# A fused embed, attention and mixture-of-experts kernel: image 2 moved behind tile 1's first gate, image 3's maxima moved to block 5, image 1's reciprocal moved to VectorE

## The chip, the cores and the metric

The kernel runs on one core of a Trainium2 chip. The metric is the device time of one execution in microseconds (us). The engines are TensorE (PE; its weight loads are PEld), VectorE (DVE), ScalarE (ACT), GpSimd (POOL) and SyncE (SP), which here only issues transfers. Each engine works through its own list of instructions in order and waits on semaphores that other engines or transfers raise.

## The reference, cut to what matters

16 images, each of 36 patch tokens and 77 text tokens (113 in all), width 192.

```python
h = embed(x)                       # patches @ proj_w.T + proj_b
h = concat([h, txt], axis=1)       # 16 x 113 x 192
h = h + attn(layernorm(h))         # 12 heads of 16; the mask bars token i >= 1 from itself
h = h + ffn(layernorm(h))

def ffn(u):                        # u: 1808 tokens x 192
    pe = softmax(posembed @ pos_w + pos_b)
    y = moe_mlp(u, sg_w, su_w, sd_w)                       # shared expert, 384 hidden
    for i in range(16):
        f = u * pe[i] @ gate_w + gate_b                    # 192 values for each token
        weight, idx = top_k(f, 96)
        weight = softmax(weight)
        g = take_along_axis(u, idx) * weight               # 96 of the token's own columns
        y = y + moe_mlp(g, eg_w[i], eu_w[i], ed_w[i])
    yn = layernorm(y, eps=1e-6) * ln_g + ln_b
    return silu(yn @ m1_w + m1_b) @ m2_w + m2_b
```

The expensive part is the top 96 of 192 values in descending order, for 16 experts and 1808 tokens.

## The kernel before, in words

The 1808 tokens are one rest tile of 16 tokens (tile 0) and 14 tiles of 128 (tiles 1 to 14). A tile's 16 experts are taken four at a time; such a unit of work is a **block**. Block 0 is the rest tile (its 16 experts lie packed in two bands of 128 rows), blocks 1 to 56 are tiles 1 to 14 with g = 0 to 3.

**VectorE's share of a block** (`slot` in `block.vector`, L626 on): for each pair of experts, 12 rounds. A round finds, for two experts, the next eight largest values (L643), their indices (L647) and strikes them out (L649). A block has 2 x 12 rounds, block 0 has 12. After round 0 of the next block `close_block` (L624) writes the low digits of the indices: until then nobody may use block n's indices. Before a block's pair VectorE waits for its gate values (`keys`), and for `weights_ready`, that is, for the exponentials of the block two before it. Between rounds it also takes the maxima of the attention scores of later images (L593, three instructions per image); `max_after` says behind which round, as (block, pair, round).

**The rest of the pipeline.** The other engines work on a block in 16 steps (octets); (n, o) below is step o of block n. In each step TensorE makes a one-hot code from the index digits (L1269), looks tokens up with it (L1281), ScalarE copies both out (L834, L844), GpSimd multiplies them (L1113). Beside that fixed work a step may hold a gate (L1245: gate values of a later block, copied to `keys` by ScalarE at L793, the next step), an expert unit going up (L1330, L1335, L1338) or, four steps later, down (L1362), the closing of a tile, or one attention stage. At step 8 of block n-1 ScalarE takes block n's indices (`prepare`, L809 to L811); GpSimd squares them, SyncE sends them to DRAM and back into `rows`, and TensorE needs these rows at step 14 of block n-1.

**Attention.** The 15 stages of an image are embed, turn_x, q, k, v, s0 to s2 (scores), t0 to t2 (turned probabilities), mix, turn_o, proj, turn_h. The images 0 and 1, and image 2 up to its scores, run ahead of block 0 in the order of the list `FIRST`; `FIRST_MORE` says behind which stage ScalarE does a stage's second half (the squares of a layer norm, the exponentials of the scores). The rest of image 2 and images 3 to 15 stand in the steps of the blocks: `attention_steps` gives each stage the next step that is free by `FREE`, with a minimal distance (`GAP`, else 2). Tile 1 needs images 0 and 1 whole, so its first gate stands behind (1, "turn_h"); tile 2 needs image 2.

In TensorE's list the three early gates (0,1), (1,0), (1,1) of tile 1 stood behind (2, "s2"). ScalarE's (1, "turn_h") copied first to `hst` and then to `nt_gate`, which the gate reads. Image 1's softmax sums were inverted by GpSimd with a power (L1014).

SyncE's list matters at one place: in block 1's slot it loads expert weights, waits for the first unit to be down (`downed`), and only behind these loads issues the digits of block 2 (L490) and their return (L498).

## Time and profile before

| | us |
|---|---|
| median of 3 runs | 2607.87 |
| lowest and highest | 2597.53, 2609.46 |
| the profiled execution itself | 2605.05 |
| its span, first to last instruction | 2603.2 |
| mean granted TensorE clock | 0.907 |

How to read it: busy time is counted inside the span. A clock of 1.00 is 2.4 GHz, 0.50 is 1.2 GHz. Idle time of an engine is put down to what released it. The chain is followed back from the last instruction, at each step to what released it. So it names the work that a later end would need, while an idle stretch that is not on it may cost nothing.

### The profile page before, as it was taken

Reading aid. Unit: us, or ns where it says so; the run is one execution under the profiler, and the core shown is the slowest. Engines: PE = TensorE matmul, PEld = TensorE weight load, DVE = VectorE, ACT = ScalarE, POOL = GpSimd, SP = SyncE. Lnnn points to the kernel's source line nnn. Section 1 sums busy time; section 2 is a strip of 40 time slices with the busy share of each in tenths; the row PEclk is TensorE's granted clock in tenths of the full one; section 3 lists DMA queues with packets and bytes.
Section 4 is the critical chain, followed back from the end, with each engine's and each line's share of the span. In section 5 each row is a group of like instructions: output and inputs, shape, how many; then the busy total and the mean of one; then the engine's idle time right before and its main releaser. Section 6 shows DMA issues by size and latency. Waiting matters only on the chain.

```text
span 2603.2 us, 48218 instructions
## 1 busy us (share of the span) xinstructions
PE 2285.7 (88%) x11466; PEld 1244.9 (48%) x11466; DVE 2494.4 (96%) x13314; ACT 1701.2 (65%) x4090; POOL 1791.9 (69%) x2165
## 2 busy tenths in 40 slices
PE   6788989999988889889998889899889988887888
PEld 4555545454444454445544445445445454443445
DVE  5897999999999999999999999999999999999983
ACT  3354676776776667676667767667676666666563
POOL 1245777777786677777767777767768777676683
PEclk8688999988999799999899999998998988989798
DMA  3021222222221222221222122222221222121211
GB/s 107 18 56 27 53 52 61 46 50 55 53 62 44 47 58 46 57 56 44 53 52 61 45 53 50 57 50 56 51 53 49 46 50 61 43 57 46 50 50 26
DMA packets 124767, 133.58 MB, mean 51 GB/s; under 512 B 39923, under 2 KB 112638, under 8 KB 124486
## 3 DMA queue, kind: packets, MB, share of 16 engines
q1 hardware_dynamic: 123174, 128.02, 21.1%
q8 instruction: 95, 1.56, 0.3%
q14 instruction: 186, 1.52, 0.2%
q0 software_dynamic: 880, 1.62, 0.2%
q10 hardware_dynamic: 432, 0.86, 0.1%
HBM read 102.58 MB, written 27.87 MB: 50 GB/s over the span
## 4 chain that ended last, share of the span: by engine, by line
DVE 74%; PE 12%; DMA 4%; POOL 4%; ACT 3%; issue 3%; SPq 0%; DVEq 0%; ACTq 0%; POOLq 0%
DVE idx L647 26%; DVE keys L649 25%; DVE vals L643 22%; PE ps L1281 3%; DMA rows<-digit_d 2%; PE ps L1338 1%; PE ps L1362 1%; DMA digit_d<-dcode 1%; PE ps L1294 1%; PE ps L1245 1%; PE ps L1269 1%; POOL picked L1113 1%; ACT code L834 1%; DVE nmax L593 1%; PE ps L1335 1%
## 5 line engine op out<-in xcount | busy, mean ns | idle before, releaser
L1113 POOL TENSOR_TENSOR picked<-looked_s,code 128x384 f32<-128x384 f32 (+1 forms) x896 | 878.9, 990 | 456.6 <-ACT looked_s L844 455.2
L647 DVE FIND_INDEX8 idx<-vals,keys 128x8 uint16<-128x192 f32 x2712 | 943.2, 349 | 0.0
L844 ACT ACTIVATE looked_s<-ps 128x384 f32<-128x384 f32 (+1 forms) x896 | 440.6, 492 | 653.6 <-PE ps L1281 651.6
L649 DVE MATCH_REPLACE8 keys<-vals,keys 128x192 f32<-128x192 f32 x2486 | 843.4, 339 | 0.0
L643 DVE MAX8 vals<-keys 128x8 f32<-128x192 f32 x2712 | 822.3, 343 | 19.3 <-ACT keys L793 19.3
L1281 PE MATMUL ps<-code,table 128*128 128x384 f32 (+1 forms) x1824 | 839.0, 544 | 0.0
L834 ACT ACTIVATE code<-ps 128x768 f32<-128x768 f32 (+1 forms) x896 | 725.7, 810 | 69.1 <-PE ps L1269 60.4
L1269 PE MATMUL ps<-rows,codew 17*128 17x384 bf16 (+1 forms) x1824 | 320.1, 348 | 189.3 <-ACT code L834 115.0
L1269 PEld LDWEIGHTS ps<-rows,codew 17*128 17x128 bf16 x1824 | 86.9, 92 | 744.8 <-ACT code L834 374.7
L1281 PEld LDWEIGHTS ps<-code,table 128*128 128x128 f32 x1824 | 315.3, 205 | 190.6 <-issue 147.6
L1338 PE MATMUL ps<-xwt,wexp 96*96 96x128 f32 x1792 | 270.8, 299 | 35.9 <-ACT xwt L800 33.6
L1338 PEld LDWEIGHTS ps<-xwt,wexp 96*96 96x96 f32 x1792 | 220.3, 175 | 111.2 <-ACT xwt L800 47.4
L1043 POOL TENSOR_TENSOR prod_s<-gu_s 96x256 f32<-96x256 f32 x252 | 181.7, 721 | 95.7 <-ACT gu_s L886 94.9
L1294 PE MATMUL ps<-picked,place 128*32 128x384 f32 (+1 forms) x1824 | 220.3, 559 | 17.8 <-POOL picked L1113 17.8
L1362 PE MATMUL ps<-wdown,hid 96*128 96x192 f32 (+1 forms) x944 | 220.3, 362 | 3.2 <-POOL hid L1049 3.1
L647 DVE MATCH_VALUE_LOAD idx<-vals,keys 128x8 f32 x2712 | 199.3, 74 | 0.0
L1046 POOL TENSOR_TENSOR turned_s<-prod_s,tanh_s 96x256 f32<-96x256 f32 x252 | 181.5, 720 | 19.8
L1049 POOL TENSOR_TENSOR hid<-prod_s,turned_s 96x256 f32<-96x256 f32 x252 | 181.3, 719 | 19.8
L1245 PE MATMUL ps<-wgate,nt_gate 96*128 96x384 f32 x448 | 187.1, 543 | 4.4 <-ACT nt_gate L768 1.7
L1362 PEld LDWEIGHTS ps<-wdown,hid 96*128 96x128 f32 (+1 forms) x944 | 161.9, 200 | 41.5 <-issue 23.7
L649 DVE MATCH_VALUE_LOAD keys<-vals,keys 128x8 f32 x2486 | 170.6, 69 | 0.0
L886 ACT ACTIVATE gu_s<-ps 96x512 f32<-96x512 f32 x250 | 150.7, 603 | 0.0
(166 smaller groups left out, 2228.3 us busy)
## 6 DMA issues: line engine op xcount, KB each, us to landing
wexp<-in_w_exp SPq DMA_DIRECT2D x58, 576.0 KB, 4.3
wdown<-in_w_down SPq DMA_DIRECT2D x58, 576.0 KB, 4.5
digit_d<-dcode SPq DMA_DIRECT2D x56, 384.0 KB, 2.6
rows<-digit_d SPq DMA_DIRECT2D x224, 96.0 KB
table<-norm_d SPq DMA_DIRECT2D x448, 3.0 KB
patch<-in_patches SPq DMA_DIRECT2D x16, 108.0 KB, 4.7
norm_d<-hs SPq DMA_DIRECT2D x16, 84.8 KB
tok_d<-h SPq DMA_DIRECT2D x16, 84.8 KB
```

The source lines that it names most:

```text
L643: nc.vector.max(vals[:, par, e, at], from_keys[:, e, :]).then_inc(chain, 1)
L647: found = nc.vector.max_index(idx[:, par, e, at], vals[:, par, e, at], from_keys[:, e, :])
L649: nc.vector.match_replace(from_keys[:, e, :], vals[:, par, e, at], from_keys[:, e, :], NEG).then_inc(chain, 1)
L834: nc.scalar.activation(code[:, o % 4, :, 0:w], ps[:, CODE_B:CODE_B + 2, 0:w], ACT.Relu).then_inc(code_ready, 1)
L844: nc.scalar.activation(looked_s[:, o % 4, 0:w], ps[:, LOOK_B[o % 2], 0:w], ACT.Copy).then_inc(looked_out, 1)
L1113: nc.gpsimd.tensor_tensor(picked[:, o % PICKS, w], looked_s[:, o % 4, w], code[:, o % 4, 1, w], ALU.mult).then_inc(picked_ready, 1)
L1245: ins = nc.tensor.matmul(ps[:, bank, 0:2 * D], nt_gate[0:HALF + k, k, :], wgate[0:HALF + k, k, GRP * g + 2 * pair:GRP * g + 2 * pair + 2, ...
L1269: ins = nc.tensor.matmul(ps[:, CODE_B + a, w], codew[at, :], rows[at, octet(o), w], start=True, stop=True)
L1281: ins = nc.tensor.matmul(ps[:, LOOK_B[o % 2], w], table[:, o, :], code[:, o % 4, 0, w], start=True, stop=True)
L1294: ins = nc.tensor.matmul(ps[32 * q:32 * (q + 1), XG_B, w], place[:, r, :], picked[:, (QUADS * r + q) % PICKS, w], start=(r == 0), stop=(r ...
L1338: ins = nc.tensor.matmul(dst, wexp[:, e // GRP % 2, e % GRP, at:at + HALF], xwt[:, e % GRP, :], start=True, stop=True)
L1362: ins = nc.tensor.matmul(ps[0:REST if rest_tile else TILE, Y_B, 0:D], source[:, c, own], w, start=(u == 0 and x == 0 and c == 0), stop=(u ...
```

## The change

Five edits.

1. `FIRST`: image 1's embed moves from ahead of (0, "turn_x") to behind (0, "v"). Image 2's stages, which lay between those of image 1, all move behind (1, "turn_h"), and with it behind tile 1's first gate. The other three early gates now stand inside image 2 (behind its embed and turn_x). The rest tile's gate (`gate_rest`, `keys_out(0, 0, 0)`) moves from behind (0, "turn_h") to behind (1, "s0").
2. Image 2's exponentials move from the end of `FIRST` to steps 0 to 2 of block 0, so its t0 moves from (0, 0) to (0, 4); with it every stage of images 2 to 5 moves by 2 to 12 steps. For image 3: embed (0, 14) to (1, 7), s0 to s2 from (1, 13), (1, 15), (2, 1) to (2, 5), (2, 7), (2, 13). From image 6 on nothing moves.
3. `max_after`: image 2's maxima from (1, 0, 4) to (1, 0, 9), image 3's from (3, 1, 9) to (5, 0, 3), image 4's from (6, 1, 9) to (7, 0, 9), image 5's from (10, 0, 6) to (10, 1, 0).
4. Image 1's sums are inverted by VectorE behind round 8 of block 0 with a reciprocal, no longer by GpSimd.
5. ScalarE: a one-element copy ahead of all others, so that the table load no longer follows TensorE's first result; the exponential for `pe` moves from behind (0, "q") to behind (0, "k"); at (1, "turn_h") the copy to `nt_gate` comes first.

TensorE's list around tile 1's first gate (L1245 before, L1259 after; `v,probt` is image 1's mix, `wpatch,patch` an embed). Before:

```order
L1225 MATMUL ps<-v,probt 113x17 x12
L1198 MATMUL ps<-xt,wqk 128x113 x6
L1188 MATMUL ps<-ident,xn 96x113 x2
L1233 MATMUL ps<-wo,ot 113x192 x2
L1234 MATMUL ps<-h,ident 113x192
L1198 MATMUL ps<-xt,wqk 128x113 x6
L1206 MATMUL ps<-wv,xt 113x192 x2
L1188 MATMUL ps<-ident,hs 96x113 x2
L1245 MATMUL ps<-wgate,nt_gate 128x384 x2
```

After:

```order
L1239 MATMUL ps<-v,probt 113x17 x12
L1202 MATMUL ps<-ident,xn 96x113 x2
L1247 MATMUL ps<-wo,ot 113x192 x2
L1248 MATMUL ps<-h,ident 113x192
L1202 MATMUL ps<-ident,hs 96x113 x2
L1259 MATMUL ps<-wgate,nt_gate 128x384 x2
L1188 MATMUL ps<-text,ident 113x192
L1193 MATMUL ps<-wpatch,patch 36x192 x6
L1194 MATMUL ps<-bpatch,ones 113x192
```

Image 2's q, k and v are gone from between image 1's mix and the gate, and its embed follows the gate.

ScalarE's list at the same place (`hs,stat` is the square for image 1's second norm, `keys` the gate's result). Before:

```order
L780 ACTIVATE hs,stat<-h,stat 113x192
L735 ACTIVATE kz<-ps 32x3x113 x4
L739 ACTIVATE v<-ps 113x12x16
L764 ACTIVATE hst<-ps 96x226
L768 ACTIVATE nt_gate<-ps 96x2x31
L793 ACTIVATE keys<-ps 128x384
```

After:

```order
L791 ACTIVATE hs,stat<-h,stat 113x192
L772 ACTIVATE nt_gate<-ps 96x2x31
L778 ACTIVATE hst<-ps 96x226
L804 ACTIVATE keys<-ps 128x384
L820 ACTIVATE dcode<-digits 128x192
```

Five copies no longer stand ahead of the one to `nt_gate`.

TensorE's list at step (0, 14), where the first code of block 1 (384 wide) is made (`picked,place` is fixed work). Before:

```order
L1269 MATMUL ps<-rows,codew 128x384 x2
L1294 MATMUL ps<-picked,place 32x192 x4
L1174 MATMUL ps<-text,ident 113x192
L1179 MATMUL ps<-wpatch,patch 36x192 x6
L1180 MATMUL ps<-bpatch,ones 113x192
L1281 MATMUL ps<-code,table 128x192
```

After:

```order
L1283 MATMUL ps<-rows,codew 128x384 x2
L1308 MATMUL ps<-picked,place 32x192 x4
L1202 MATMUL ps<-ident,xn 96x113 x2
L1295 MATMUL ps<-code,table 128x192
```

Image 3's embed has left this step, and image 2's turn_o has come.

The diff, cut to what decides the order:

```diff
-FIRST = [(0, "embed"), (1, "embed"), (0, "turn_x"), (0, "q"), (0, "k"), (0, "v"), (1, "turn_x"), (0, "s0"), (0, "s1"), (0, "s2"),
...
+FIRST = [(0, "embed"), (0, "turn_x"), (0, "q"), (0, "k"), (0, "v"), (1, "embed"), (0, "s0"), (0, "s1"), (0, "s2"),
...
+REST_OF = STAGES[STAGES.index("t0"):]
@@ attention_steps
+        if i < AHEAD:
+            step = 3 - GAP[REST_OF[0]] + 1
         for stage in REST_OF if i < AHEAD else STAGES:
-            if stage not in ("embed", "t0") or stage == "t0" and i >= AHEAD:
+            if stage != "embed":
@@ ATT_MORE
+for _c in range(3):
+    ATT_MORE[AHEAD - 1, f"s{_c}"] = _c
@@ max_after
-    spots = {(0, 0, 2): 1, (1, 0, 4): 2}
+    spots = {(0, 0, 2): 1, (1, 0, 9): 2}
...
-        block, r = divmod(rounds, 2 * ROUNDS)
+        block, r = divmod(rounds + (ROUNDS if i == AHEAD else 0), 2 * ROUNDS)
@@ VectorE, slot
+                            if (n, pair, r) == (0, 0, 8):
+                                dve.wait_ge(misc_out, stage_out(1, "mix"))
+                                nc.vector.reciprocal(rinv[:], mix[:, :, DH]).then_inc(att_rinv, 1)
@@ ScalarE, attend_out, turn_h
+                        if i == 1:
+                            to_gate()
+                            act.wait_ge(packed, 2)
+                        nc.scalar.activation(hst[:], turn_view(i, stage), ACT.Copy).then_inc(misc_out, 1)
+                        if i == 0:
+                            to_gate()
@@ ScalarE, the list
+                nc.scalar.activation(nmax[0:1, 0:1], ones[0:1, 0:1], ACT.Copy)
...
-                    if (i, stage) == (0, "q"):
+                    if (i, stage) == (0, "k"):
                         act.wait_ge(pe_max, 1)
...
-                    if (i, stage) == (0, "turn_h"):
+                    if (i, stage) == (1, "s0"):
                         keys_out(0, 0, 0)
...
-                    if (i, stage) == (2, "s2"):
-                        for g, pair in ((0, 1), (1, 0), (1, 1)):
-                            keys_out(1, g, pair)
+                    if (i, stage) == (2, "embed"):
+                        keys_out(1, 0, 1)
+                        keys_out(1, 1, 0)
+                    if (i, stage) == (2, "turn_x"):
+                        keys_out(1, 1, 1)
@@ GpSimd, attend, mix
-                        if i:
+                        if i >= 2:
@@ TensorE, the list: the same three places as ScalarE's
```

## Rows read from the trace of the kernel before

**Rows 1.** The page's part 1: busy us (share of the span) and instructions.
```profile
PE 2285.7 (88%) x11466; PEld 1244.9 (48%) x11466; DVE 2494.4 (96%) x13314; ACT 1701.2 (65%) x4090; POOL 1791.9 (69%) x2165
```

**Rows 2.** VectorE's timeline: start, us, line, tiles, [idle before <- what ended it].
```profile
69.64 0.61 DVE L643 MAX8 vals<-keys 128x8 f32<-128x192 f32 x2
...
71.47 0.61 DVE L643 MAX8 vals<-keys 128x8 f32<-128x192 f32 x2
...
84.95 0.62 DVE L643 MAX8 vals<-keys 128x8 f32<-128x192 f32 x2 [8.31 <-ACT keys L793]
...
223.10 0.62 DVE L593 TENSOR_REDUCE nmax<-score 113x4 f32<-113x452 f32 x1 [10.93 <-ACT score L742]
229.87 0.62 DVE L593 TENSOR_REDUCE nmax<-score 113x4 f32<-113x452 f32 x1 [6.14 <-ACT score L742]
```

**Rows 3.** The chain that ended last, 131 to 240 us: start, us, what.
```profile
131.65 0.52 ACT whole L810
...
163.50 6.82 PE ps L1335 x64
...
180.23 5.32 PE ps L1362 x32
...
186.87 8.58 DMA digit_d<-dcode
...
197.38 5.00 DMA rows<-digit_d
...
204.36 10.35 PE ps L1335 x64
```

**Rows 4.** The same chain, 585 to 640 us.
```profile
625.35 0.39 ACT keys L793
625.76 0.61 DVE vals L643 x2
```

**Rows 5.** The same chain, 626 to 2545 us, grouped by line.
```profile
by line: DVE idx L647 34.6%; DVE keys L649 33.4%; DVE vals L643 28.4%; issue 1.0%; DVE nmax L593 0.8%; DVE digits L624 0.8%; PE ps L1281 0.3%; DVEq L625 0.1%; PE ps L1269 0.1%; PE ps L1338 0.1%; PE ps L1294 0.1%; PE ps L1362 0.1%; ACT code 
```

**Rows 6.** Timelines of ScalarE and VectorE at tile 3's first gate.
```profile
449.00 0.50 ACT L793 ACTIVATE keys<-ps 128x384 f32<-128x384 f32 x1
...
451.28 0.60 DVE L643 MAX8 vals<-keys 128x8 f32<-128x192 f32 x2
```

**Rows 7.** Timelines of GpSimd and ScalarE ahead of tile 1's first gate.
```profile
70.43 2.28 POOL L1014 TENSOR_TENSOR rinv<-mix,powers 113x12 f32<-113x12 f32 x1 [5.59 <-ACT mix L751]
...
79.12 0.50 POOL L1033 TENSOR_SCALAR hs<-h,stat 113x192 f32<-113x192 f32 x1
...
79.21 1.82 ACT L735 ACTIVATE kz<-ps 32x339 f32<-32x339 f32 x4 [1.09 <-PE ps L1198]
...
81.52 0.22 ACT L768 ACTIVATE nt_gate<-ps 96x62 f32<-96x62 f32 x1
```

**Rows 8.** TensorE's timeline: embed twice, a proj, a k, a score.
```profile
56.43 2.14 PE L1179 MATMUL ps<-wpatch,patch 128*36 128x192 f32 x12
...
136.67 1.62 PE L1233 MATMUL ps<-wo,ot 128*113 128x192 f32 x4
...
146.97 3.89 PE L1179 MATMUL ps<-wpatch,patch 128*36 128x192 f32 x12
...
185.46 1.59 PE L1198 MATMUL ps<-xt,wqk 128*128 128x113 f32 x12
...
195.01 0.92 PE L1214 MATMUL ps<-kz,qt 128*113 128x452 f32 x2
```

**Rows 9.** Stages: stretch, us, busy us of each engine, TensorE's granted clock, DMA.
```profile
99.00:131.00 32.00, 26.48 (x98) 16.49 (x98) 32.00 (x176) 10.20 (x26) 8.78 (x12) 0.50 0.02 3
...
152.00:202.00 50.00, 43.57 (x261) 25.28 (x259) 50.00 (x274) 26.30 (x67) 24.32 (x33) 0.93 0.27 66
202.00:223.00 21.00, 20.58 (x98) 13.52 (x99) 10.18 (x54) 4.86 (x9) 4.16 (x5) 0.52 0.10 24
223.00:626.00 403.00, 365.21 (x1885) 199.95 (x1884) 395.63 (x2122) 280.34 (x679) 302.90 (x366) 0.93 0.22 51
```

More of the change, by code:

```diff
@@ L69 @@
         2: [1, 5, 7, 9, 11, 13, 15], 3: [1, 5, 7, 9, 11, 13, 15]}
-FIRST = [(0, "embed"), (1, "embed"), (0, "turn_x"), (0, "q"), (0, "k"), (0, "v"), (1, "turn_x"), (0, "s0"), (0, "s1"), (0, "s2"),
[3 rows of a table removed]
-FIRST_MORE = {(0, "turn_x"): [(1, "embed")], (0, "s1"): [(0, "s0")], (0, "s2"): [(0, "s1"), (0, "s2")],
-              (1, "s1"): [(1, "s0")], (1, "s2"): [(1, "s1"), (1, "s2")], (2, "s2"): [(2, "s0"), (2, "s1"), (2, "s2")]}
-REST_OF = ["t0", "t1", "t2", "mix", "turn_o", "proj", "turn_h"]
+FIRST = [(0, "embed"), (0, "turn_x"), (0, "q"), (0, "k"), (0, "v"), (1, "embed"), (0, "s0"), (0, "s1"), (0, "s2"),
[3 rows of a table added]
+FIRST_MORE = {(0, "s0"): [(1, "embed")], (0, "s1"): [(0, "s0")], (1, "turn_x"): [(0, "s1"), (0, "s2")], (1, "s1"): [(1, "s0")],
+              (1, "s2"): [(1, "s1"), (1, "s2")]}
+REST_OF = STAGES[STAGES.index("t0"):]
 FIRST_BANKS = [2, XG_B, GU_B, CODE_B, CODE_B + 1, 1]
@@ L761, in attend_out, with to_gate @@
                             act.wait_ge(normt_out, 16 * i)
-                        if i == 1:
-                            act.wait_ge(packed, 2)
-                        nc.scalar.activation(hst[:], turn_view(i, stage), ACT.Copy).then_inc(misc_out, 1)
-                        if i < 2:
+                        def to_gate():
                             mine, at = (slice(REST, TOK), 0) if i == 0 else (slice(0, REST + TILE - TOK), TOK - REST)
@@ L1431, in _ @@
                         ins.then_inc(pe_mm, 1)
-                    if (i, stage) == (0, "turn_h"):
+                    if (i, stage) == (1, "s0"):
                         pe.wait_ge(pe_col_ready, 1)
@@ L1440, in _ @@
                         gate(1, 0, 0)
-                    if (i, stage) == (2, "s2"):
-                        for g, pair in ((0, 1), (1, 0), (1, 1)):
-                            gate(1, g, pair)
+                    if (i, stage) == (2, "embed"):
+                        gate(1, 0, 1)
+                        gate(1, 1, 0)
+                    if (i, stage) == (2, "turn_x"):
+                        gate(1, 1, 1)
                 pe.wait_ge(placed_w, 5 + PER // 2)
```

6 rows, old and new, of the table FIRST are left out of this document.

## The prediction, as it was put on record

> **What bounds the kernel now.** I read the page's busy shares first: VectorE is busy 96% of the span [rows 1], so at first sight only VectorE's idle time is to be had. Its own timeline shows where that lies [rows 2]: 8.31 us ahead of block 1, and 10.93 + 6.14 = 17.07 us in block 3, where it waits for image 3's scores. The change addresses both, and a reader who stops here forecasts 17 us and more.
>
> The chain of waits says something else. It has three parts. Up to 131 us it ends in VectorE, whose indices of block 1 ScalarE takes at 131.65. From there to 625.8 us it isn't in VectorE at all: it goes through TensorE, ScalarE, GpSimd and the transfers of the digits and rows [rows 3, 4], and leaves them only where ScalarE has copied tile 4's first gate values and VectorE starts block 13, at 625.76. From there to 2545 us it is VectorE in over 96% [rows 5]. The 17.07 us lie in the middle part, at 212 to 230, beside the chain and not on it. Two more rows show that VectorE may not use the time if it gets it. Tile 3's first gate values are copied at 449.00 to 449.50, and VectorE begins them at 451.28 [rows 6]: it could come 1.8 us earlier there and no more. At block 13 it is already too early. In the middle part TensorE is busy 365.21 of 403 us (91%) [rows 9]: this pipeline runs at its own pace, and VectorE's stall of 17 us has been absorbed by it before block 13. So the question is by how much the pipeline comes to block 13 earlier, not by how much VectorE does.
>
> **The change part by part.**
>
> Start, image 0. Image 1's embed and its copy leave the way of image 0's, and the table load goes ahead. I cost both at nothing up to image 0's scores, because ScalarE must copy the mask behind (0, "turn_x") in both kernels, and the mask's transfer doesn't move; what comes earlier waits there. Moving the `pe` exponential behind k saves less than 1 us of ScalarE, and image 1's turn_x and q, now ahead of image 0's t0, take about as much back.
>
> Tile 1's first gate. The reciprocal: GpSimd's power ends at 70.43 + 2.28 = 72.71 [rows 7]. VectorE's comes behind round 8 of block 0, which runs from 69.64 to 71.47 [rows 2] (so a round is 1.83 us), and with one short instruction ends by 71.7: 1.0 us earlier. It isn't 2.3 earlier, since the reciprocal must wait for its place between rounds. Then the norm that ended at 79.12 + 0.50 = 79.62 ends at 78.6, and TensorE's turn_h, about 0.6, at 79.3. The copy to `nt_gate` stood at 81.52, behind image 2's k (79.21 to 81.03), v and `hst` [rows 7]; now it follows at once, at 79.4. The gate and its copy follow in both, so VectorE, which began block 1 at 84.95, begins it 2.2 us earlier, at 82.8. Bounds: 0, if image 1 comes later by as much, and 8.31, the whole wait. I take 2.2 because every link but one is a row.
>
> Image 2 then stands behind the gate. TensorE reaches block 0 at about 101 instead of 99, but ScalarE waits for block 1's indices until 131.65 anyway, and those come with VectorE, 2.2 us earlier. The shift of the chain at 131 is -2.2.
>
> Block 0's end. At (0, 14) TensorE has waited for the rows of block 1, and everything behind is on the chain. Image 3's embed stood there, 3.89 us at half clock for its larger part [rows 8]; two short transposes replace it: -3.9. Image 2's mix comes from (0, 6) to (0, 10), ahead of that wait, which covers it.
>
> Block 1 up to the unit at step 9. proj comes in at (1, 1): +1.6 at half clock. The embed at (1, 7) takes the place of a q: 2.14 at full clock for 1.59 [rows 8], +0.6. The clock is a cost of its own. Before, the embed at 146.97 ran at half clock and the stretch from 152 on had 0.93 [rows 8, 9]. Without the embed the first steps of block 1 may stay at half clock. Until the gate and the proj are through that is 0 to 4 us; I take 2. Here SyncE issues block 2's digits only when the unit that ends at 185.55 is down [rows 3], so what the pipeline gains up to there is kept by the transfers (186.87 to 202.4). Shift there: -2.2 - 3.9 + 1.6 + 0.6 + 2.0 = -1.9.
>
> Blocks 1 to 10. Image 3's k, v and s0 stood ahead of the wait for block 2's rows and now stand behind it: 1.59 + about 0.8 + 0.92 = +3.3 [rows 8]. Stages of images 3 to 5 that fall into steps 9 to 13 of a block run while rows are awaited and cost nothing; block 8 gets such a pair. I count half of the 3.3: +1.7. Bounds 0 and 3.3. All other stages of images 3 to 5 are done by block 10 in both kernels, and image 6 stands where it stood.
>
> VectorE's maxima of image 3, in block 5, will find their scores ready, and ScalarE, which wants them at (3, 5), finds VectorE ahead by more than 10 us, since VectorE has 17.07 us more. Their 3 x 0.62 us of work remain. The reciprocal adds some 0.2 us of VectorE work ahead of block 13: nothing.
>
> Sum at block 13: -1.9 + 1.7 = -0.2 us. VectorE's list behind it is the same in both, so the end moves by the same. From the profiled execution, 2605.05 us (span 2603.2 and 1.85 around it), the forecast is **2605 us**. The median of the runs shown, 2607.87, is 2.8 above that execution, which lies inside their range; I don't correct for it.
>
> **The rivals.**
>
> A, faster: TensorE's clock stays up. The stretch from 202 to 223 ran at 0.52 with TensorE busy 20.58 of 21 us [rows 9], directly on the chain. If the new order keeps the clock up there, half of it goes, -10.3, and the 2.0 above aren't paid: -12.5, 2592.5 us. VectorE would allow it: its own limit is 17.07 + 2.2 lower, 2585.8. For it: TensorE now comes into block 0 straight from image 2's scores, without a wait. Against: the half clock at 202 follows on a wait for rows that doesn't go away, and TensorE was busy 26.48 of 32 us from 99 to 131 at 0.50 [rows 9], so being busy did not bring the clock back. The Trainium skill, "TensorE: Matmul & The Clock Gate", section on the HAM clock gate, says that the default is the throttled state and that activity releases the throttle. By that rule block 0 would run at full clock here, and this rival would be the likeliest. The trace doesn't agree for narrow work like block 0's, where the clock stayed at 0.50. Chance 0.17.
>
> B, slower: without the embed at (0, 14) the half clock lasts through block 1. The same 64 matmuls took 6.82 us at full clock and 10.35 at half, a factor of 1.52 [rows 3]. On the 43.57 us of TensorE's work from 152 to 202 [rows 3, 9] that is +22.7. About two thirds of it lie ahead of the unit that SyncE waits for, +15; the rest is covered by the transfer. With the 2.0 above taken out the sum is -2.2 + 15, so 2618, and 2623 if some of it goes on behind 202. It decides from where the half clock outlasts step (1, 9); a clock that is back by (1, 5) costs less than 4. For it: block 0 at 0.50 for its whole length. Against: block 1's matmuls are twice as wide, and at 223 the clock came back amid such work. Chance 0.12.
>
> C, no gain at the gate: image 2's maxima at (1, 0, 9) wait. VectorE gets there at 82.8 + 10 x 1.83 = 101.1. From the gate's end, about half a us ahead of that start, TensorE has an embed, three gates, q, k, v and three scores to do and ScalarE the 1.82 of k, some 19 us at full clock, which is also 101. At half clock for all of it the scores are 8 us late, and these go into block 1's end and so onto the chain: 2605 + 8 = 2613 us. Chance 0.11.
>
> D, the change does more than I allow: the pipeline keeps VectorE's 17 us because it follows VectorE somewhere that I overlook: 2586 us. The chain between 131 and 626 has no VectorE row longer than the others, which speaks against it. It is part of A's 0.17, as 0.04.
>
> **How the numbers follow.** The forecast has 0.60. Its own range comes from the bounds: the gate 0 to -8.3 but in truth near 2.2, the clock 0 to 4, the deferred stages 0 to 3.3; together 2597 to 2612. A measurement of this kernel tells 0.5%, 13 us, from no change: faster is below about 2595, slower above 2621. A and D are faster (0.17); C and the forecast are no change (0.71); B splits between no change and slower, and with what I haven't seen slower has 0.11, no change 0.72. For 8 in 10 the range takes in A's near half and most of B: 2589 to 2617.
>
> **What would show it right or wrong.** VectorE's 10.93 and 6.14 us ahead of the maxima are gone, and new waits on `keys` or on the pipeline stand ahead of blocks 5 to 13 instead, of about the same sum: that is the main test. The wait ahead of block 1 is about 6 us instead of 8.3. Block 13 starts within a few us of 625.8. The chain changes from the pipeline to VectorE at block 13 as before. TensorE's clock from 143 to 165 decides between forecast, A and B. I am wrong if VectorE is busy without a wait from block 1 to block 13, or if block 13 starts before 612 or after 640.

## The result, and the profile after

| | before | changed |
|---|---|---|
| median, 20 runs each on one chip | 2607.79 us | 2616.36 us |
| lowest and highest | 2597.53, 2615.29 | 2601.56, 2627.34 |
| profiled execution (span, clock) | 2605.05 (2603.2, 0.907) | 2606.09 (2604.3, 0.914) |

The ratio is 1.0035, 95% interval 1.0023 to 1.0046: slower by some 9 us, inside what the prediction calls no change, but a real loss, where it put the change at -0.2. The profiled execution of the changed kernel is a lucky one, 10.3 us below its median. Over its 20 runs the median clock is 0.900, and time and clock go against each other (correlation -0.72, 9 us for each 0.01 of clock). A lower mean clock isn't the loss, though: in the second set of runs below, the median clocks of the two kernels are 0.904 and 0.9035, and the loss is 8.3 us. So the two profiles, 1.1 us of span apart, show where the waits lie, while the size of the loss comes from the many runs; no execution as slow as the changed kernel's median was profiled.

The page's part 1 of the changed kernel, beside [rows 1]:

```profile
PE 2263.2 (87%) x11466; PEld 1234.0 (47%) x11466; DVE 2494.7 (96%) x13315; ACT 1700.3 (65%) x4091; POOL 1789.3 (69%) x2164
```

VectorE does the same work (2494.4 before). VectorE's timeline at its waits, beside [rows 2]:

```profile
82.59 0.62 DVE L647 MAX8 vals<-keys 128x8 f32<-128x192 f32 x2 [6.54 <-ACT keys L804]
...
260.66 0.62 DVE L647 MAX8 vals<-keys 128x8 f32<-128x192 f32 x2 [5.61 <-ACT ew L831]
...
372.09 0.62 DVE L597 TENSOR_REDUCE nmax<-score 113x4 f32<-113x452 f32 x1 [4.77 <-ACT score L749]
375.62 0.62 DVE L597 TENSOR_REDUCE nmax<-score 113x4 f32<-113x452 f32 x1 [2.90 <-ACT score L749]
380.29 0.62 DVE L597 TENSOR_REDUCE nmax<-score 113x4 f32<-113x452 f32 x1 [4.05 <-ACT score L749]
...
454.16 0.62 DVE L647 MAX8 vals<-keys 128x8 f32<-128x192 f32 x2 [6.22 <-ACT keys L804]
```

The 17.07 us at image 3's maxima are gone. In their place stand 5.61 ahead of block 5, 11.72 at image 4's maxima in block 7 and 6.22 ahead of block 9, 23.55 in all; block 13 is no longer waited for. The chain of waits from 131 to 240 us, beside [rows 3]:

```profile
161.08 8.03 PE ps L1349 x64
...
181.19 5.32 PE ps L1376 x32
...
187.82 8.32 DMA digit_d<-dcode
...
197.65 5.02 DMA rows<-digit_d
...
204.65 10.35 PE ps L1349 x64
```

The unit that SyncE waits for ends at 186.51 (185.55 before), and block 2's rows land at 202.67 (202.38): nothing of the gain at the start has come through. The same chain, 440 to 470 us, at tile 3's first gate, beside [rows 6]:

```profile
440.65 2.48 PE ps L1239 x24
...
448.63 2.56 PE ps L1259 x4
...
453.65 0.49 ACT keys L804
454.16 0.61 DVE vals L647 x2
```

This answers to [rows 4] too: the chain leaves the pipeline for VectorE here, at block 9, and no longer at block 13. Image 4's mix (L1239) stands at step 1 of block 7 and the gate (L1259) at step 3. The keys come 4.65 us later than the 449.00 of before, where the same gate ran without the mix ahead of it and at full clock:

```profile
445.79 1.46 PE L1245 MATMUL ps<-wgate,nt_gate 96*128 96x384 f32 x4
```

Stages by the same four stretches as [rows 9]:

```profile
99.00:131.00 32.00, 19.57 (x83) 10.51 (x85) 32.00 (x169) 15.42 (x45) 7.02 (x12) 0.66 0.02 3
152.00:202.00 50.00, 43.14 (x244) 25.70 (x242) 50.00 (x274) 21.21 (x57) 22.48 (x33) 0.88 0.25 65
202.00:223.00 21.00, 20.28 (x106) 14.90 (x106) 21.00 (x115) 3.90 (x8) 3.35 (x5) 0.53 0.11 25
223.00:626.00 403.00, 363.84 (x1900) 200.09 (x1897) 379.45 (x2044) 283.47 (x687) 303.59 (x367) 0.94 0.22 51
```

In the last stretch VectorE is busy 379.45 us where it was busy 395.63: the time won by 223 us is given back as waits by 626. From 630 to 2510 us VectorE is busy 1880.00 of 1880.00 us in both kernels, so the end follows from where VectorE stands at block 13.

### The profile page after: what moved, and what is told of

Same layout as the page of the kernel before. It is cut to its first block, busy times and chain, and to the rows that moved or that the text cites. A ratio compares the mean times of both kernels' runs of the same rounds, so it can differ in the third digit from the quotient of the medians.

```text
span 2604.3 us, 48219 instructions
## 1 busy us (share of the span) xinstructions
PE 2263.2 (87%) x11466; PEld 1234.0 (47%) x11466; DVE 2494.7 (96%) x13315; ACT 1700.3 (65%) x4091; POOL 1789.3 (69%) x2164
## 4 chain that ended last, share of the span: by engine, by line
DVE 81%; PE 9%; DMA 3%; ACT 2%; issue 2%; POOL 2%; SPq 0%; DVEq 0%; ACTq 0%; POOLq 0%
DVE idx L651 29%; DVE keys L653 28%; DVE vals L647 24%; PE ps L1295 2%; DMA rows<-digit_d 1%; PE ps L1376 1%; DMA digit_d<-dcode 1%; PE ps L1352 1%; DVE nmax L597 1%; DVE digits L628 1%; PE ps L1349 1%; PE ps L1308 1%; PE ps L1283 1%; PE ps L1259 1%; DMA wv<-in_w_v 1%
## 5 line engine op out<-in xcount | busy, mean ns | idle before, releaser
L1295 PE MATMUL ps<-code,table 128*128 128x384 f32 (+1 forms) x1824 | 830.2, 538 | 0.0
L1376 PE MATMUL ps<-wdown,hid 96*128 96x192 f32 (+1 forms) x944 | 215.0, 355 | 2.9 <-POOL hid L1063 2.9
L1259 PE MATMUL ps<-wgate,nt_gate 96*128 96x384 f32 x448 | 188.5, 546 | 3.0 <-ACT gu_s L897 1.4
```

Of the source, the lines that this page charges most:

```text
L1259: ins = nc.tensor.matmul(ps[:, bank, 0:2 * D], nt_gate[0:HALF + k, k, :], wgate[0:HALF + k, k, GRP * g + 2 * pair:GRP * g + 2 * pair + 2, ...
L1295: ins = nc.tensor.matmul(ps[:, LOOK_B[o % 2], w], table[:, o, :], code[:, o % 4, 0, w], start=True, stop=True)
L1376: ins = nc.tensor.matmul(ps[0:REST if rest_tile else TILE, Y_B, 0:D], source[:, c, own], w, start=(u == 0 and x == 0 and c == 0), stop=(u ...
```

## The experiments

Twelve kernels were run on three occasions, each beside the kernel before (2605.63, 2604.7 and 2606.13 us). The letters in the expectations don't mean the same throughout. In the first set (start_only to early_gate) P says that the end is set by when the first gates of tiles 3 and 4 are ready, and that the later steps delay them, and V that every wait of VectorE counts at the end. In the last set (t0_gate_max, mix_after_gate, early_gate_max4) P says that each wait of VectorE comes from a place in the written order, and V that TensorE's pipeline is late as a whole, so that a wait taken away comes back at the next thing VectorE meets. The ratio is to the kernel before in the same set, with its 95% interval; it isn't the quotient of the two medians.

**start_only**: the new start, with the old steps of the attention stages and the old place of image 3's maxima.

```
-         if i < AHEAD:
-             step = 3 - GAP[REST_OF[0]] + 1
-         block, r = divmod(rounds + (ROUNDS if i == AHEAD else 0), 2 * ROUNDS)
+         block, r = divmod(rounds, 2 * ROUNDS)
```

> Edits 1, 4 and 5 of the change alone: the new order up to block 0, with the attention steps, image 3's to 5's maxima and the place of image 2's exponentials (end of the list ahead of block 0) as before. Theory P (the end is set by when TensorE's pipeline hands VectorE the first gate of tile 3 or 4; the later steps of images 3 to 5 put more of their work ahead of tile 3's gate, and this is what costs): without the later steps the loss goes; ratio to before 0.998 to 1.001, VectorE's 17 us at image 3's maxima are back, no wait at block 9, block 13 starts within 3 us of 625.8. Rival S (the new start costs, since TensorE enters block 0 later and at another clock): ratio 1.003 or more here too. Rival V (every wait of VectorE counts): the wait at image 3's maxima is back in place of 23.5 us of new ones, so about 0.998.

Measured: 2610.88 us, ratio 1.0018 (1.0008 to 1.0027). VectorE's timeline:

```profile
224.37 0.62 DVE L593 TENSOR_REDUCE nmax<-score 113x4 f32<-113x452 f32 x1 [14.68 <-ACT score L745]
230.79 0.62 DVE L593 TENSOR_REDUCE nmax<-score 113x4 f32<-113x452 f32 x1 [5.80 <-ACT score L745]
```

The two waits add up to 20.5 us, 3.4 more than in [rows 2], while VectorE had begun block 1 2.5 us sooner (82.45). VectorE waits 0.16 us at block 9 and is at the same place at block 13 as before (its digits at 627.27 against 627.60), as P had it. The ratio lies between P's range and S's and is clear of 1: the start alone gains nothing and costs some 5 us, about half of the whole loss. The profile doesn't show where, since it is that of the fastest of the 12 runs (2604.76).

**steps_only**: the other half, the new steps and maxima with the old start.

```
+         if i < AHEAD:
+             step = 3 - GAP[REST_OF[0]] + 1
-         block, r = divmod(rounds, 2 * ROUNDS)
+         block, r = divmod(rounds + (ROUNDS if i == AHEAD else 0), 2 * ROUNDS)
```

> Edits 2 and 3 alone, on the kernel before: the old order ahead of block 0, image 2's exponentials in steps 0 to 2, all stages of images 2 to 5 in their later steps, maxima of images 3 to 5 in their new places, image 2's at (1, 0, 4). Theory P: this part carries the loss; ratio 1.003 to 1.006, the first wait of VectorE behind block 5 that counts stands at block 9 on keys, with block 9 starting 3 to 10 us later than in the kernel before (451.3). Rival S: ratio 1.000. Rival V: VectorE waits as long as in the changed kernel and starts 2.3 us later, so about 1.004 as well; only its waits tell it from P.

Measured: 2617.31 us, ratio 1.0039 (1.0024 to 1.0053), span 2618.4. VectorE's waits from 84 to 630 us:

```profile
DVE nmax L597 <- ACT score L746: 18.0, 3, 11.0
DVE vals L647 <- ACT keys L797: 8.7, 1, 8.7
DVE vals L647 <- ACT ew L824: 7.7, 2, 7.1
```

34.4 us in place of 18.2, with the span 15.2 longer, in the slowest of the six runs: what this run loses is paid as VectorE's waits. The ratio is P's and S falls. The way is P's in part: block 9 begins at 465.81, 14.5 us later than before and not 3 to 10, and the larger waits, 18.0 us, come earlier, at image 4's maxima in block 7. The two halves don't add up: the steps cost more with the old start (1.0039) than with the new one (1.0035 against 1.0018).

**max4_late**: the changed kernel with image 4's maxima later, at round 4 of the second pair of block 7.

```
+         if i == AHEAD + 1:
+             block, r = 7, ROUNDS + 4
```

> The changed kernel with image 4's maxima taken behind round 4 of block 7's second pair, where the scores are ready, instead of behind round 9 of the first pair, where VectorE waited 11.7 us. Theory P: the 11.7 us turn up as a longer wait for keys at block 9 (6.2 becomes about 18), block 9 starts at the same time, and the ratio to before stays at 1.0035, within 0.001. Rival V: the kernel is 11.7 us faster than the changed one, ratio 0.999.

Measured: 2611.34 us, ratio 1.0029 (1.0014 to 1.0044). VectorE's timeline at block 9:

```profile
451.30 0.62 DVE L649 MAX8 vals<-keys 128x8 f32<-128x192 f32 x2 [17.78 <-ACT keys L806]
```

The 11.7 us at the maxima are gone, and the wait ahead of block 9 has grown from 6.2 to 17.8; block 9 begins 2.9 us earlier. The wait moved, P's case.

**early_gate**: the changed kernel with each tile's gates one place earlier in the order (tile 3's first from step 3 of block 7 to step 12 of block 6), and the load of the gate's input one block earlier.

```
- GATE_SPOTS = {0: {1: (3, 0), 3: (3, 1)}, 1: {}, 2: {3: (0, 0), ...
+ GATE_SPOTS = {0: {1: (3, 1)}, 1: {12: (0, 0)}, 2: {3: (0, 1), ...
```

> The changed kernel with the gates of each tile from tile 3 on moved up: the first gate of tile t+1 from step 3 of its g = 2 block to step 12 of the g = 1 block, the others each to the place of the one ahead of them, the load of the gate's input one block earlier. Same work. Theory P: the wait at block 9 (6.2 us) and what stands in other runs for it go, VectorE keeps its lead over the pipeline, and the end comes earlier by at least that: ratio to before 0.992 to 0.999, and no wait for keys from block 9 on. If VectorE alone set the end behind block 9 and its lead were worth nothing, the ratio stays at 1.0035.

Measured: 2607.62 us, ratio 1.0003 (0.9989 to 1.0016). The wait ahead of block 9 is gone; 16.0 us stand at image 4's maxima and 5.3 at image 5's, and 6.0 ahead of block 5. That gives back most of the loss, at the median, and misses P's range (0.992 to 0.999) by a little. The profile is of the slowest of the 12 runs (2618.44).

**after_again**: the changed kernel as it is, in the second set.

> The changed kernel itself, for a second profile and as the anchor of this set of runs. Its first profiled execution, 2606.09 us, lay near the low end of its runs (2601.56 to 2627.34). Theory P (the pipeline, which hands VectorE the first gates of tiles 3 and 4 late, sets the time): ratio 1.003 to 1.004; an execution near the median has its extra time ahead of block 9 or 13, as a later start of that block behind a wait for keys, at a lower TensorE clock between 300 and 450 us, and VectorE's time from block 13 on is the same. Rival E (the extra time lies in the later blocks or the tail): blocks 9 and 13 start where they did in the first profile, and the end is later.

Measured: 2613.0 us, ratio 1.0032 (1.0019 to 1.0044), VectorE's waits 24.6 us (15.1 at image 4's maxima, 6.2 ahead of block 5, 3.3 ahead of block 9): the result repeats. The profiled execution, 2608.16 us, is again faster than the median, so that it doesn't decide between P and E. Against the first profile block 12's digits are 1.3 us later (629.86 against 628.54), and the span is 2.0 us longer.

**early_gate_before**: the kernel before with the same earlier gates.

> The kernel before with the gates of each tile moved up as in early_gate. Theory P: VectorE has no lead in block 9 here, since it lost 17 us at image 3's maxima, so the earlier gate gives only what it waited for keys at block 13 (1.1 us in the profile, perhaps 5 us in slower runs): ratio 0.998 to 1.000, and VectorE's 17 us at image 3's maxima now count. Rival G (the place of the gates is itself worth the 8 us that early_gate has over the changed kernel, whatever the rest): ratio 0.996 to 0.997.

Measured: 2605.03 us, ratio 1.0005 (0.999 to 1.0019). Its 15.3 us of waits at image 3's maxima stay. Earlier gates alone are worth nothing to the kernel before, and G falls.

**early_gate_max**: early_gate with the maxima of images 4 and on later by some rounds.

```
+         if i >= 7:
+             block, r = divmod(rounds + 3, 2 * ROUNDS)
+         if i in {4: (7, 16), 5: (10, 20), 6: (14, 3)}:
+             block, r = {4: (7, 16), 5: (10, 20), 6: (14, 3)}[i]
```

> early_gate, with image 4's, 5's and 6's maxima 7, 8 and 6 rounds later and those of images 7 to 15 three rounds later, so that VectorE finds its scores ready while it leads. In early_gate VectorE waited 16.0 us for image 4's and 5.3 us for image 5's. Theory P with the gates moved: these waits are now on the chain, and without them VectorE is held only by the exponentials of the block two before it, so of the 21 us 8 to 20 come back: ratio 0.992 to 0.997. Rival Q (the pipeline as a whole, not its gates, sets the pace up to block 13): the waits turn up elsewhere (exponentials, keys of other blocks), ratio 1.000.

Measured: 2596.29 us, ratio 0.9966 (0.9951 to 0.9981), faster than both kernels and inside P's range; Q falls. All that is left of the waits stands ahead of block 5, where early_gate waited 6.0 us:

```profile
DVE vals L652 <- ACT ew L836: 8.4, 1, 8.4
```

**t0_at_2**: the changed kernel with image 2's t0 at step 2 of block 0 and not at 4, and what follows from it: image 4's t0 to mix at (5, 15) to (6, 7), and mix no longer in block 7.

```
-             step = 3 - GAP[REST_OF[0]] + 1
+             step = 3 - GAP[REST_OF[0]] - 1
```

> The changed kernel with image 2's first turn of the probabilities at step 2 of block 0 instead of 4, which pulls images 2 to 5 forward by two to eight steps (image 3's turn_o from (4, 1) to (3, 13), image 4's mix from (7, 1) to (6, 7)), with the maxima of images 3 to 5 forward as the planner has them. A dose of edit 2 between none and all. Theory P with the later steps as its cause: ratio between 1.000 and 1.003, tile 3's first gate earlier than in the changed kernel (453.8). If the later steps are not the cause (only the new start is): ratio 1.0035, as the changed kernel.

Measured: 2599.03 us, ratio 0.9977 (0.9964 to 0.9991), outside what was expected, on the good side. On the same chip the changed kernel took 2613.0. Two steps in one number are worth 14 us. Tile 3's first keys are copied at 448.84 and not at 453.65, and VectorE waits 17.3 us from block 1 to block 13 (23.5 in the changed kernel). The start is the changed kernel's, so the steps are a cause. The time doesn't simply grow with the delay: with the old steps (start_only) the ratio is 1.0018, with this delay 0.9977, with the whole 1.0035.

**t0_gate_max**: the last two together (image 4's maxima at round 2 of the second pair of block 7).

> The changed kernel with three alterations together: image 2's t0 at step 2 of block 0 and not 4 (alone 2599.0 us), the gates of tiles 3 and on one place earlier, and the maxima of images 4 and on later (these two alone 2596.3 us). Theory P (what is lost is lost at VectorE's waits in blocks 4 to 9, which each come from a place in the written order): the waits between 131 and 626 us, 17 us in the run with t0 at step 2 and 8.4 us in the run with the gates and maxima, fall below 5 us, and the time is 2590 to 2595 us. Rival V (the TensorE pipeline has so much to do that a wait taken away at one place comes back at another): the waits add up to 8 us or more again, some of them ahead of blocks 9, 13 or 17, and the time is 2596 to 2600 us.

Measured: 2587.5 us, ratio 0.993 (0.9908 to 0.9951), the best of all and better than P's 2590 to 2595; V falls. Its waits from 84 to 630 us, the first of which is the one ahead of block 1, and the stretch from 84 to 2510 us:

```profile
DVE vals L652 <- ACT keys L809: 6.5, 1, 6.5
DVE nmax L602 <- ACT score L754: 0.5, 1, 0.5
```

```profile
84.00:2510.00 2426.00, 2155.25 (x10962) 1168.52 (x10961) 2424.95 (x13084) 1645.26 (x3927) 1750.53 (x2099) 0.92 0.22 51
```

The columns are the stretch, its us, then busy us of TensorE, its weight loads, VectorE, ScalarE and GpSimd, the clock and the DMA. VectorE is busy 2424.95 of 2426.00 us. TensorE's clock over nearly the same stretch (84 to 2530 us) is 0.92 in the changed kernel too, so the gain isn't one of the clock.

**mix_after_gate**: the changed kernel with image 4's mix four steps later, behind tile 3's first gate.

```
-                 step += GAP.get(stage, 2)
+                 step += GAP.get(stage, 2) + (4 if (i, stage) == (4, "mix") else 0)
```

> The changed kernel with image 4's mix four steps later, from step 1 of block 7 to step 5, so that it stands behind tile 3's first gate at step 3 (its turn_o, proj and turn_h and the stages of image 5 follow it by four steps or so); the rest is as in the changed kernel. Theory P: tile 3's keys come 3 to 4 us earlier (the mix took 2.5 us of products at half clock right ahead of the gate), the wait ahead of block 9, 6.2 us in the changed kernel, is 2 to 3 us, the 11.7 us at image 4's maxima stay, and the time is 2609 to 2613 us. Rival V: the wait ahead of block 9 stays within 1 us of 6.2 and the time at 2613 to 2617 us. Rival K (half clock around step 2 of block 7, which has its cause ahead in block 6, sets it): the gate comes early in the order and is as late in time, because its own products run at half clock.

Measured: 2610.03 us, ratio 1.0012 (1.0 to 1.0023). The chain at the gate:

```profile
450.76 1.29 PE ps L1259 x4
...
453.93 0.39 ACT keys L804
```

The gate's products take 1.29 us (2.56 at half clock in the changed kernel), but the keys are no earlier. TensorE's mean clock from the landing of block 7's rows to the gate is 0.64, and the lookup just ahead of block 7 begins 4.4 us later than in the changed kernel (442.05 against 437.68). That is what rival K said of the half clock around step 2, though not of the gate's own products. The wait ahead of block 9 is 4.0, more than the 3.3 of the changed kernel's second profile, and the waits add up to 25.6. So P's time came without P's mechanism, and the interval overlaps that of the changed kernel. The expectation also puts the changed kernel's mix at half clock; it took 2.5 us at a clock of 1.00 (438 to 442 us).

**early_gate_max4**: early_gate with image 4's maxima alone later.

> The changed kernel with the gates one place earlier and the maxima of image 4 alone later, at round 4 of the second pair of block 7 (the run before this one moved those of images 5 and on as well and took 2596.3 us; gates alone 2607.6 us). Theory P: 16.0 us of waits at image 4's maxima go and about 5.6 us ahead of block 5 stay, with those at image 5's maxima (5.3 us with the gates alone) or a few more, so 2598 to 2602 us. Rival V: the 16 us come back at block 9 or at image 5's maxima, and the time is 2606 us or more.

Measured: 2610.02 us, ratio 1.0007 (0.9991 to 1.0023): V's case. VectorE's timeline at image 5's maxima:

```profile
514.19 0.62 DVE L600 TENSOR_REDUCE nmax<-score 113x4 f32<-113x452 f32 x1 [6.89 <-ACT score L752]
519.59 0.62 DVE L600 TENSOR_REDUCE nmax<-score 113x4 f32<-113x452 f32 x1 [4.77 <-ACT score L752]
524.47 0.62 DVE L600 TENSOR_REDUCE nmax<-score 113x4 f32<-113x452 f32 x1 [4.26 <-ACT score L752]
```

15.9 us stand one image further on, at image 5's maxima, which had not been moved.

**before_gate_max**: the kernel before with earlier gates and later maxima.

```
+         if i in {3: (4, 10), 4: (6, 22), 5: (10, 12), 6: (14, 3)}:
+             block, r = {3: (4, 10), 4: (6, 22), 5: (10, 12), 6: (14, 3)}[i]
```

> The kernel before with the gates one place earlier and the maxima of image 3 one block later (round 10 of the first pair of block 4), those of images 4 to 6 and on later by 1 to 6 rounds: what the kernel before gains from the same treatment as gave the changed kernel 2596.3 us. Theory S (the changed kernel's start is worth something, hidden by its waits): the 17.0 us at image 3's maxima go, a wait of about 6 us ahead of block 5 or 9 comes, and the time is 2599 to 2603 us, 3 to 7 us above the changed kernel so treated. Rival N (the start's edits are worth nothing on the whole; the treatment alone gives the gain): 2594 to 2598 us, the same as the changed kernel so treated.

Measured: 2604.33 us, ratio 0.998 (0.9965 to 0.9994), 1.3 us above S's numbers. As S said, the 17 us at image 3's maxima are gone: the three run together at 235.62 us without a wait. But the wait moved here too: 12.0 us (2.50, 4.18 and 5.30, at 350 to 361 us) stand at image 4's maxima in block 6, and 0.8 ahead of block 5, 12.8 in all. By the medians this treatment brings the kernel before 2 us and the changed one 17 (2613.0 to 2596.3); by the ratios they end at 0.998 and 0.9966, whose intervals overlap. So N's time is missed, but a gain of the changed kernel's start over that of the kernel before isn't shown. It wasn't tried whether other places for the maxima would bring the kernel before more.

The waits of VectorE between block 1 and block 13, its busy time and the span, in each profiled execution:

| kernel | waits, us | VectorE busy, us | span, us | span less both |
|---|---|---|---|---|
| before | 18.2 | 2494.4 | 2603.2 | 90.6 |
| changed | 23.5 | 2494.7 | 2604.3 | 86.1 |
| changed, again | 24.6 | 2494.1 | 2606.3 | 87.6 |
| start_only | 20.7 | 2493.8 | 2602.9 | 88.4 |
| steps_only | 34.4 | 2496.6 | 2618.4 | 87.4 |
| max4_late | 21.0 | 2494.5 | 2607.1 | 91.6 |
| early_gate | 27.3 | 2499.2 | 2616.6 | 90.1 |
| early_gate_before | 15.3 | 2497.3 | 2602.9 | 90.3 |
| early_gate_max | 8.4 | 2497.9 | 2596.8 | 90.5 |
| t0_at_2 | 17.3 | 2493.5 | 2596.3 | 85.5 |
| t0_gate_max | 0.5 | 2493.7 | 2581.9 | 87.7 |
| mix_after_gate | 25.6 | 2496.0 | 2606.7 | 85.1 |
| early_gate_max4 | 26.5 | 2493.7 | 2609.7 | 89.5 |
| before_gate_max | 12.8 | 2502.4 | 2605.3 | 90.1 |

The last column is VectorE's idle time ahead of block 1 and behind block 56 (in max4_late with 3.5 us more of waiting at 2016 us). It spreads over 6.5 us, the busy time over 9 and the waits over 34, so in these executions the large differences of span are differences of the waits, whichever engine the chain of waits names. For differences of a few us, as between the kernel before and the changed one, all three count.

## Why the prediction was wrong

**Start, image 0; tile 1's first gate**: right. VectorE begins block 1 at 82.59 (82.8 forecast), its wait is 6.54 ("about 6"). The links are right too: the reciprocal is done at 71.02 (71.7), the norm at 78.00 (78.6), the copy to `nt_gate` begins at 78.77 (79.4).

**Image 2 then stands behind the gate; block 0's end; block 1**: the shift of -2.2 at 131 came (-2.4) and was lost on TensorE. Ahead of the 64 matmuls of step 5 it is still -2.4 (161.08 against 163.50), where the sum, -2.2 - 3.9 + 1.6 + 2.0, has -2.5; at the unit of step 9 it is +1.0 and not -1.9. So the miss of 2.9 lies behind 161.08. TensorE's busy time and granted clock in stretches of 4 us, first before, then changed:

```profile
144.00:148.00 4.00, 3.18 (x16) 0.50 0.00 0
148.00:152.00 4.00, 4.00 (x16) 0.68 0.02 4
152.00:156.00 4.00, 3.94 (x22) 1.00 0.07 8
...
160.00:164.00 4.00, 3.52 (x17) 1.00 0.00 0
164.00:168.00 4.00, 4.00 (x48) 0.95 0.00 0
```

```profile
144.00:148.00 4.00, 4.00 (x17) 0.50 0.05 5
148.00:152.00 4.00, 4.00 (x8) 0.50 0.08 8
152.00:156.00 4.00, 3.93 (x14) 0.80 0.01 2
...
160.00:164.00 4.00, 3.52 (x37) 0.98 0.00 0
164.00:168.00 4.00, 4.00 (x27) 0.50 0.00 0
```

The half clock lasts some 3 us longer, which the 2.0 covered. Then the clock falls back some 4 us earlier than before, so that the 64 matmuls take 8.03 us and not the 6.82 of [rows 3]: 1.2 us that no term had. The other 1.6 us of the miss lie between them and the unit's end. The largest part is that the sum took an embed as its `wpatch` products alone. It has two more groups on the chain:

```profile
174.52 0.51 PE ps L1188 x2
175.03 2.07 PE ps L1193 x12
177.10 0.51 PE ps L1194 x2
```

The sum left the same two groups out where the embed goes from step (0, 14), which is a gain that it didn't count. That it is right at 161.08 is in part luck.

The transfers hid it: block 2's rows are 0.3 us later. So at block 2 the gain of the start is gone, and nothing is lost beyond it. Of the rivals, A fell (0.53 at 202 to 223 us, as before), B too (full clock by 156, so well before step 9), and so did C: VectorE takes image 2's maxima at 100.88 us without a wait.

**Blocks 1 to 10**: this step failed. It said that the stages of images 3 to 5 that fall behind cost half of 3.3 us, that those in steps 9 to 13 "run while rows are awaited and cost nothing", and that "all other stages of images 3 to 5 are done by block 10 in both kernels". The last is true and doesn't matter. VectorE doesn't meet them at block 10 or 13. It meets image 4's scores in block 7, where it lost 11.7 us that no term had, and tile 3's gate ahead of block 9, where the keys were 4.65 us late against a term of +1.7 with an upper bound of 3.3. Ahead of block 5 it waits 5.6 us for the exponentials of the block two before it, which no term had either. The section on the change had the moves too small as well: image 4's t2, mix, turn_o, proj and turn_h move by 14 to 16 steps and not by up to 12 (image 5's turn_h by none). Its t0, t1 and t2 go from steps 11, 13 and 15 of block 5 to steps 5, 7 and 13 of block 6, and its mix from step 1 of block 6 to step 1 of block 7, 8 us ahead of the gate that VectorE waits for next.

The mix isn't all of the 4.65 us, and the clock is the part that the prediction had no term for here. For tile 3's first gate, how long TensorE waited for block 7's rows, the time from there to the gate's products, and the clock in that time:

| kernel | wait for rows, us | rows to gate, us | clock | image 4's mix between |
|---|---|---|---|---|
| before | 1.24 | 11.3 | 1.00 | no |
| t0_at_2 | 0.81 | 11.6 | 1.00 | no |
| start_only | 1.60 | 13.0 | 0.87 | no |
| changed, again | 2.66 | 14.7 | 0.88 | yes, 2.55 us |
| mix_after_gate | 2.88 | 16.8 | 0.64 | no |
| changed | 3.13 | 18.3 | 0.69 | yes, 2.55 us |
| max4_late | 2.56 | 18.5 | 0.68 | yes |

In the changed kernel the rows are even there 4.3 us earlier than before (430.11 against 434.45), and the way from there to the gate is 7.0 us longer: 2.55 are the mix, the rest goes with the lower clock. The clock stayed at 1.00 in the two kernels with the shortest waits for the rows and was below 0.9 in the others. That the wait brought it down, and what lengthens the wait, wasn't tried.

steps_only shows the waits with the old start (34.4 us). max4_late and early_gate_max4 show that no single place is the cause; t0_at_2 shows that the places as a whole are one. How much each stage costs by itself stays open: mix_after_gate moved one of them, and its keys were no earlier. So does the loss of some 5 us in start_only, where the steps are the old ones: the prediction's terms for the start have no loss in them, and the one profile of that kernel shows none.

**The sum at block 13** rested on reading the chain between 131 and 626 us as the only path. "VectorE's stall of 17 us has been absorbed by [the pipeline] before block 13" was so in that execution, since block 13 waited 1.1 us for its keys. But the slack was that small: VectorE was 1.8 us behind the keys at block 9 and 1.1 ahead of them at block 13, and two paths that close each bound the time. A delay of 4.65 us at block 9 therefore came straight onto VectorE's path and stayed there, where the prediction had priced it only at block 13. The main test of the prediction, that waits of about the same sum take the place of the 17, was met (23.5 for 18.2). Their surplus of 5.3 us, less the 2.4 gained at block 1, should give +2.9; block 12's digits are 0.9 later in the profile, since VectorE's own work up to there took 2.1 us less in that execution. In the medians the loss is 9 us. The profiles account for the waits that came and for 1 us of that loss; the other 8 belong to slower executions than those profiled, and where in them they lie isn't shown.

**Rival D**, the pipeline follows, was given 0.04 and 2586 us, and the changed kernel isn't it. Yet 2585.8, VectorE's own limit by the prediction, is near where t0_gate_max arrived: 2587.5 us. The argument that VectorE may not use the time if it gets it held only for the gates and maxima where they stood.

## What to carry to other kernels

When a wait is taken from the engine that is busy 96%, list what that engine waits for next in its own order, each with its slack, and price every moved stage, and the clock that it may cost, at the first of these, not at the point where the chain happened to change engines. Two paths within 2 us of each other both bound the time. A wait that moves from place to place needs its whole row of places moved together: gates, image 4's maxima, or both gave 2608 to 2611 us here, gates and the maxima of all images from 4 on 2596, and with image 2's t0 two steps earlier as well, and the stages that follow from it, 2587.5.

## What the hardware showed unexpectedly

One execution is a poor judge of a change of 9 us: the changed kernel's 20 runs spread over 26 us, and its profile came from the one with the highest clock of the 20 (0.914; the lowest is 0.896). In the 11 runs of after_again time and clock hardly go together (correlation -0.20), so the clock explains only some of the spread.

A busy TensorE didn't mean a faster clock. TensorE in stretches of 8 us of block 0, first before, then changed (the columns are busy us, clock, DMA share, GB/s):

```profile
107.00:115.00 8.00, 8.00 (x32) 0.50 0.01 3
115.00:123.00 8.00, 8.00 (x31) 0.50 0.02 3
```

```profile
107.00:115.00 8.00, 8.00 (x31) 0.50 0.01 3
115.00:123.00 8.00, 5.03 (x26) 0.93 0.06 6
```

After 8 us without a gap at half clock the kernel before stayed there through 8 more such, while the changed kernel got the full clock with other stages in the same place (image 2's mix runs from 114.3 to 119.1 us in the kernel before, and from 131.6 us in the changed one). The Trainium skill, "TensorE: Matmul & The Clock Gate", section on the HAM clock gate, says that activity releases the throttle. The changed kernel's rows go with that, those of before don't.

An instruction of one shape hasn't one price. VectorE's digits, of which 56 of 57 have the same shape, in the kernel before (columns: least, median and greatest ns):

```profile
L624 DVE TENSOR_SCALAR digits<-idx x57: 210/255/2715, 76.4 to 2530.0; 128x384 uint16<-128x384 uint16 x56, 128x192 uint16<-128x192 uint16 x1
```

The greatest is ten times the median: 2.7 us at once on the engine that sets the time. The trace shows what goes with it. VectorE and GpSimd at that place:

```profile
278.04 2.71 DVE L624 TENSOR_SCALAR digits<-idx 128x384 uint16<-128x384 uint16 x1
...
277.75 2.89 POOL L1113 TENSOR_TENSOR picked<-looked_s,code 128x384 f32<-128x384 f32 x3
```

GpSimd was already at work when the digits began, and they ended at 280.75, 0.11 us behind GpSimd's last product. The same holds for all 15 digits in the kernel before that took over 0.45 us: each began while GpSimd ran an instruction and ended 0.11 to 0.13 us behind the end of one. The maxima, indices and strikes beside it don't lengthen so. It adds up: over the 14 profiled executions the digits take 24.0 to 33.2 us, and VectorE's busy time without them is 2468.3 to 2469.7. So nearly all of the 9 us by which VectorE's own work differs from one of these kernels to the next is this one instruction. That GpSimd holds it up is read from these times; a run that keeps the two apart wasn't made.
